# Contextual position attention in a decoder layer: selection in two halves, the position term added by VectorE, the table one group ahead

## The reference, cut to what matters

```
logits   = Q K^T / sqrt(32)
gates    = sigmoid(logits)
pos      = min(reverse cumulative sum of gates over the keys, 63)
table    = Q pos_emb                      # 64 values for each query
cope     = linear interpolation of table at pos
out      = softmax(logits + cope) V
```

## Time and profile before

| What | us |
|---|---|
| three runs, median (lowest to highest) | 15981.76 (15937.47 to 16006.48) |
| the profiled execution, own time | 15948.25 |
| its span, first to last instruction | 15946.6 |
| PE busy in the span | 13087.7 (82%) |
| VectorE (DVE) busy | 7428.1 (47%) |
| GpSimd (POOL) busy | 6506.6 (41%) |
| ScalarE (ACT) busy | 4470.2 (28%) |

### The profile page before, as it was taken

The page is one execution under the profiler, slowest core; times in us unless marked ns, Lnnn a source line. Parts: engine busy times, 40 slices in busy tenths (PEclk is TensorE's granted clock), DMA queues, the critical chain, the costliest instruction groups (busy, mean ns, idle before and its releaser), DMA issues. The chain is left out here.

```text
span 15946.6 us, 176609 instructions
## 1 busy us (share of the span) xinstructions
PE 13087.7 (82%) x57462; PEld 8694.1 (55%) x57462; DVE 7428.1 (47%) x13140; ACT 4470.2 (28%) x7890; POOL 6506.6 (41%) x5384
## 2 busy tenths in 40 slices
PE   8788999998668888888888888888888888888755
PEld 3553333333446666666666666666666666666622
DVE  0112222222235555555555555555555555555533
ACT  0111222221123333333333333333333333333310
POOL 0000000000026666666666666666666666666500
PEclk9888888898778888888888888888888888888866
DMA  3111000001123333333333333333333333333313
GB/s 79 46 44 26 20 20 20 20 20 32 64 62 76 76 74 74 77 78 74 76 75 75 75 78 78 75 77 74 75 74 77 78 75 76 75 75 75 74 63 100
DMA packets 1037897, 1029.79 MB, mean 65 GB/s; under 512 B 738307, under 2 KB 845571, under 8 KB 972307
## 3 DMA queue, kind: packets, MB, share of 16 engines
q1 hardware_dynamic: 964114, 1020.70, 27.1%
q10 hardware_dynamic: 73728, 8.42, 0.4%
HBM read 817.83 MB, written 210.76 MB: 65 GB/s over the span
## 5 line engine op out<-in xcount | busy, mean ns | idle before, releaser
L910 PE MATMUL c_pickps<-c_table,c_hot 128*128 128x112 f32 x16384 | 3422.2, 386 | 894.3 <-DMA c_table<-t_tables 795.5
L910 PEld LDWEIGHTS c_pickps<-c_table,c_hot 128*128 128x128 f32 x16384 | 3271.7, 258 | 985.5 <-DVE c_over L1196 872.4
L1286 POOL TENSOR_TENSOR c_total<-c_total,c_over 128x384 f32<-128x384 f32 (+3 forms) x3584 | 3282.1, 916 | 1029.8 <-DVE c_over L1196 751.4
L1286 POOL TENSOR_TENSOR c_total<-c_total,c_middle 128x1024 f32<-128x1024 f32 x512 | 1211.0, 2365 | 2944.7 <-DVE c_middle L1187 2944.7
L1173 DVE COPY_PREDICATED c_pickps<-c_upper,c_pickps 128x256 f32<-128x256 uint32 (+1 forms) x1024 | 798.9, 826 | 3042.5 <-PE c_pickps L910 3042.5
L1253 POOL IOTA c_digitrow<- 1x128 f32 x1 | 0.3, 256 | 4590.9 <-POOLq L65 4590.9
L1041 ACT ACTIVATE c_over<-c_place,c_thresholds 128x384 f32<-128x384 f32 (+3 forms) x3584 | 1589.7, 525 | 1.5 <-POOL c_place L1274 1.5
L1196 DVE TENSOR_TENSOR c_over<-c_over,c_pickps 128x384 f32<-128x384 f32 (+3 forms) x3584 | 1407.1, 452 | 0.0
L949 PEld LDWEIGHTS c_softps<-c_v,c_probs 128*128 128x128 f32 x8192 | 1206.4, 230 | 285.6 <-issue 265.2
L1024 ACT ACTIVATE c_place<-c_gateps 128x512 f32<-128x512 f32 x1024 | 608.8, 594 | 2607.5 <-PE c_gateps L885 2607.3
L949 PE MATMUL c_softps<-c_v,c_probs 128*128 128x33 f32 x8192 | 1218.4, 310 | 2.7 <-ACT c_probs L1051 2.7
(11 more groups left out here) (213 smaller groups left out, 14864.4 us busy)
## 6 DMA issues: line engine op xcount, KB each, us to landing
c_hot<-t_digits SPq DMA_DIRECT2D x512, 1024.0 KB
t_tables<-c_tablesb SPq DMA_DIRECT2D x256, 256.0 KB, 2.4
c_table<-t_tables SPq DMA_DIRECT2D x1024, 56.0 KB, 8.0
c_kb<-t_kb SPq DMA_DIRECT2D x256, 128.0 KB, 6.1
t_digits<-c_anchorrows SPq DMA_DIRECT2D x128, 256.0 KB, 2.3
a_q<-t_qa SPq DMA_DIRECT2D x128, 128.0 KB, 2.4
a_k<-t_ka SPq DMA_DIRECT2D x128, 128.0 KB, 2.5
c_ka<-t_kb SPq DMA_DIRECT2D x128, 128.0 KB, 2.3
```

The source lines that it names most:

```text
L910: mm = nc.tensor.matmul(pick_ps[:, h // 4, 0:WIDTH, r * 8:(r + 1) * 8], hot[t % 2][:, h, :], table[s][:, :, :, t * 16 + h].rearrange("p l ...
L1286: nc.gpsimd.tensor_tensor(a, a, b, ALU.add).then_inc(s_add, 1)
```

## The change

It touches `build_cope_attention` alone.

1. **Halves.** `pick`, `mux`, `product` and `gather_up` take a `part`: 0 is the first 64 queries of a step (two banks of `pick_ps`), 1 the others. Each has half the instructions (`pick`) or half the columns. `pick` of a half waits for the products of the same half of the step before.
2. **The position term.** `add_cope` goes. `top` begins with an addition of `total` to `score_ps` by VectorE, 128 x 1024, and the maximum waits for it.
3. **Tables a group earlier.** `tables`, `keep_table`, `send_tables` and `load_table` of group i+2 run in step 3 of group i, where they ran in steps 1 to 3 for group i+1. `tables` reads `q_a` in plain order, and `keep_table` reads PSUM in steps of eight columns to make the same layout. `load_table` comes behind both hot loads.
4. **Orders.** VectorE: `mux` and nine products of part 0, `compare(n+1)`, `top(n-1)`, `mux` of part 1, `top_row`, products 0 and 1 of part 1, `less`, in step 2 `near`, products 2 to 8 of part 1, `recip`. TensorE: `pick` part 1 of this step, a piece, `pick` part 0 of the next step, `turn_peak`, a piece, `bases`, a piece, `places`, `logits`, a piece, `values`, `turn_anchor`, a piece. Five gates stand in step 0, three in step 1, the two tables in step 3. ScalarE: three `aside`s with `keep_base` behind the second, in step 1 `lift`, `expo`, two `aside`s, in step 0 `lift`, `past`, `keep_anchor`, `norm`.

```diff
             def load_a(i, s):
-                after(sp, s_tableps, 2 * i)
+                after(sp, s_gateps, 8 * i)
...
             def load_table(i, s):
+                after(sp, s_pickps, 8 * i - 8)
+                sp.sem_inc(s_tablefree, 1)
                 sp.wait_ge(s_tablerows, 32 * (i + 1))
-                after(sp, s_pickps, 4 * i - 4)
...
                 if not final(i):
-                    send_tables(i + 1, 1 - s)
                     send_digits(i + 1, 1 - s)
                     load_hot(i + 1, 1 - s, 0)
-                    load_table(i + 1, 1 - s)
                     load_hot(i + 1, 1 - s, 1)
+                if not final(i, 2):
+                    send_tables(i + 2, s)
+                    load_table(i + 2, s)
...
             def tables(i, n):
...
-                nc.tensor.matmul(gate_ps[:, :].rearrange("p (l x) -> p l x", l=8), knots[:, 8 * n:8 * n + 8, :].rearrange("p m a -> p (m a)"),
-                                 q_a[:, :].rearrange("p (x l) -> p l x", l=8), start=True, stop=True).then_inc(s_tableps, 1)
+                nc.tensor.matmul(gate_ps[:, :], knots[:, 8 * n:8 * n + 8, :].rearrange("p m a -> p (m a)"), q_a[:, :],
+                                 start=True, stop=True).then_inc(s_tableps, 1)
...
-            def pick(i, s, t):
+            def pick(i, s, t, part):
                 n = 4 * i + t
-                pe.wait_ge(s_hot, n + 1)
-                if t == 0:
-                    pe.wait_ge(s_tableload, 128 * (i + 1))
-                after(pe, s_prod, PRODUCTS * n)
-                for h in range(16):
+                if part == 0:
+                    pe.wait_ge(s_hot, n + 1)
+                    if t == 0:
+                        pe.wait_ge(s_tableload, 128 * (i + 1))
+                after(pe, s_prod, PRODUCTS * (2 * n + part - 1))
+                for h in range(8 * part, 8 * part + 8):
...
             def pieces(i, t, at):
-                k = 6 * t + at
-                if k < 8:
-                    gates(i, k)
-                elif k < 10:
-                    tables(i, k - 8)
+                if t == 0 and at < 5 and not final(i):
+                    gates(i + 1, at)
+                elif t == 1 and at < 3 and not final(i):
+                    gates(i + 1, at + 5)
+                elif t == 3 and at < 2 and not final(i, 2):
+                    tables(i + 2, at)
...
-                nc.scalar.activation(table_sb[n][:, :], gate_ps[:, :], ACT.Copy).then_inc(s_tablesb, 1)
+                nc.scalar.activation(table_sb[n][:, :].rearrange("p (l x) -> p l x", l=8), gate_ps[:, :].rearrange("p (x l) -> p l x", l=8),
+                                     ACT.Copy).then_inc(s_tablesb, 1)
...
                     aside(0)
                     aside(1)
                     if behind:
                         keep_base(n - 1, 1 - x)
+                    aside(2)
                     if t == 1 and ahead:
                         lift(i + 1, 1 - s, 1)
-                    aside(2)
                     if behind:
                         expo(n - 1, 1 - x)
                     aside(3)
+                    aside(4)
                     if t == 0 and ahead:
                         lift(i + 1, 1 - s, 0)
                     if t < 3:
                         past(i, s, t + 1)
                     elif ahead:
                         past(i + 1, 1 - s, 0)
-                    aside(4)
+                    if t == 2 and ahead:
+                        keep_anchor(i + 1)
...
             def top(n, x):
+                dve.wait_ge(s_logit, n + 1)
+                dve.wait_ge(s_add, (PRODUCTS - 1) * (2 * n + 2))
+                nc.vector.tensor_tensor(score_ps[:, :, :], score_ps[:, :, :], total[x][:, :, :], ALU.add).then_inc(s_scored, 1)
                 dve.wait_ge(s_scored, n + 1)
...
-                    mux(i, s, t)
-                    if behind:
-                        top(n - 1, 1 - x)
-                    product(i, s, t, 0)
...
+                    mux(i, s, t, 0)
+                    for k in range(PRODUCTS):
+                        product(i, s, t, 0, k)
                     if t < 3:
                         compare(n + 1, 1 - x, 2 * i + (t + 1) // 2 + 1)
                     elif ahead:
                         compare(n + 1, 1 - x, 2 * i + 3)
-                    for k in range(5, PRODUCTS):
-                        product(i, s, t, k)
+                    if behind:
+                        top(n - 1, 1 - x)
+                    mux(i, s, t, 1)
+                    if behind:
+                        top_row(n - 1, 1 - x)
+                    for k in range(2):
+                        product(i, s, t, 1, k)
+                    if behind:
+                        less(n - 1, 1 - x)
                     if t == 2 and ahead:
                         near(i + 1, 1 - s)
+                    for k in range(2, PRODUCTS):
+                        product(i, s, t, 1, k)
                     if behind:
                         recip(n - 1, 1 - x)
```

More of the change, by code:

```diff
@@ L988, in step @@
                             values(n - 1, 1 - x, s)
[L989 to L998 removed]
+                    if t == 2 and ahead:
+                        turn_anchor(i + 1)
+                    pieces(i, t, 4)
+            for n in range(2):
+                tables(0, n)
             for n in range(8):
                 gates(0, n)
[L1002 to L1003 removed]
             places(0, 0)
             turn_anchor(0)
[L1006 removed]
+            for n in range(2):
+                tables(1, n)
+            pick(0, 0, 0, 0)
             quads(pe, step)
[L1008 removed]
             turn_peak(4 * last + 3, 1)
@@ L1094, in step @@
                             norm(i - 1, 1 - s, 3)
-                    aside(5)
-                    if t == 2 and ahead:
-                        keep_anchor(i + 1)
+            for n in range(2):
+                keep_table(0, n)
             for n in range(8):
@@ L1102, in _ @@
                     lift(0, 0, n // 4)
+            keep_anchor(0)
             for n in range(2):
-                keep_table(0, n)
-            keep_anchor(0)
+                keep_table(1, n)
             past(0, 0, 0)
@@ L1185, in product @@
                 elif k == 1:
-                    for b in range(4):
+                    for b in range(2):
                         ins = nc.vector.scalar_tensor_tensor(
-                            out=middle[x][:, :, b * 32:(b + 1) * 32], in0=here[:, :, b, :], scalar=-2.0,
-                            in1=pick_ps[:, b, 8, :].unsqueeze(1).to_broadcast([128, 8, 32]), op0=ALU.max, op1=ALU.mult)
+                            out=split(middle[x][:, :, mine])[:, :, b, :], in0=here[:, :, b, :], scalar=-2.0,
+                            in1=pick_ps[:, 2 * part + b, 8, :].unsqueeze(1).to_broadcast([128, 8, 32]), op0=ALU.max, op1=ALU.mult)
@@ L1300, in step @@
                         spread(i + 1, 1 - s, 0)
-                    gather_up(i, t)
+                    for part in range(2):
+                        gather_up(i, t, part)
             for k in range(LINKS):
```

140 lines of the change are left out of this document (59 added, 81 removed).

## The result

The changed kernel takes 17020.8 us (median of 4 runs, 16990.6 to 17043.4) where the kernel before takes 15994.1 on the same chip: a ratio of 1.0655, 95% interval 1.063 to 1.0679. It is slower, as forecast, but by 1027 us where 234 were forecast, and outside the range. The profiled execution has a span of 17001.0 us.

A forecast was written before the change was run, and what follows sets the result against it. No engine full, the stage runs by its waits; VectorE's chain sets the pace. Steps of 16.5, 22.0, 18.5 and 26.9 us make 83.9 a group against 82.07, +234 us: 16190 us; own range 15980 to 16450, 8 in 10 15500 to 16650.

The forecast's parts named there:

- VectorE's work: VectorE's instructions over a whole group: 55.6 us of work, 8.4 more than before.
- The hot wait: Step 3, VectorE before `compare`, for the next group's first hot load: 10.5 us idle a group, against 7.1 before.
- `over` in step 1: Product 2 of step 1: VectorE stands 4.1 us for ScalarE's `over`, late because the fifth gate's `aside` precedes `lift` and `past`.
- GpSimd: 8 more instructions a step, 9.4 us more a group: busy 60.3 of 84, hidden, not waited for at `top`.
- the 77 us: `keep_table`'s strided PSUM read on ScalarE: taken at 0.60 us; at 1.2 it would add 0.6 a group, 77 us.
- Rival C: Hot loads issued close together share their way: up to +9.4 us a group, 17380 us; at a third, 16580; chance 0.09.
- `values` on TensorE: The matmuls that `recip` waits for, at each step's end: 1.97 us, ending 4.33 after `less` starts.
- the waits before `recip`: End of each step but step 2: VectorE waits 1.7 to 4 us for TensorE's `values`.
- Those before `top_row`: VectorE before `top_row`: 1.0 us each step, because `turn_peak` is queued behind half a `pick`.
- The table a group ahead: Table's transfers leave the hot load's way: `pick` no longer waits 0.8 us a group, the load shortens by 1.0.
- The 0.8 of step 3: Step 3 after `compare`: 0.8 us added (0 to 1.4) for TensorE being slower after the pause.

The follow-up runs named there:

- The order of step 3 alone: Changed kernel with, in step 3, VectorE's `compare` moved behind `recip` and TensorE's next `pick` behind `values`: 15971.7 us, ratio 1.0008.
- parts tried alone: Kernel before with one part of the change: tables a group ahead, 15715.1 us; VectorE's addition for TensorE's product, 16794.2 us.
- the addition alone: Kernel before with VectorE adding `total` in place of TensorE's product with the identity, whole `pick`, old orders: 16794.2 us, ratio 1.0516.
- The move: 80 already met waits ahead of VectorE's and GpSimd's loops: 16971.5 us on the changed kernel, 15522.7 us with both orders mended.
- the best order: Changed kernel, ScalarE's fifth gate behind `past`, step 3's softmax before the hot wait, loop bodies moved: 15522.7 us; with TensorE's product back, 15205.6 us.

## Why the prediction was wrong

The sign and most of the mechanism held; the sum was 83.9 us a group and the chip made 90.4. By step, mean of the traces:

| step | predicted | measured | before |
|---|---|---|---|
| 0 | 16.5 | 17.3 | 18.1 |
| 1 | 22.0 | 24.2 | 19.6 |
| 2 | 18.5 | 18.1 | 17.7 |
| 3 | 26.9 | 30.8 | 26.6 |

- **VectorE's work** was right: 55.6 predicted, 56.7 measured. The 1.1 is `compare`: its mean is 1533 ns where it was 1301, over half of them still at 1.28 us and the others at up to 2.4. The long ones lie in steps 0 and 1. GpSimd is busy beside those of step 2 as well, but the long ones go with something narrower: a GpSimd operation starts while `compare` runs, 0.1 us or more from its ends. Of 253 that had such a start 228 took over 1.4 us, of the 259 others none; in the kernel before 11 of 383, and none of 129. It is a necessary mark in both traces, not a sufficient one, and no run tested it as a cause.
- **The hot wait** was right: 10.5 predicted, 1453.7/128 = 11.4. So was the reason: the softmax stands behind it. The order of step 3 alone was worth 1049 us.
- **`over` in step 1** was right: 4.1 predicted, 491.7/128 = 3.8 measured.
- **GpSimd** at 60.3 was 56.3, not waited for. `keep_table`'s strided read of PSUM took 597 ns, as the plain read of the earlier trace rows: the 77 us by the Trainium skill's rule ("SBUF — State Buffer", "Door 1: The DMA port swizzle") did not come. What that section says of strides in PSUM, it says of matmuls; it was the prediction that took it over to ScalarE. Rival C did not occur: the two hot loads went out together,

```profile
9994.99 1.32 SPq L831 DMA_DIRECT2D c_hot<-t_digits  x2
```

  and the `compare` of the first started at 10005.72, 10.7 us later, against 12.56 before.
- **The term that failed: `values` on TensorE, and so the waits before `recip`.** It is the largest part of the miss, a third of it. The prediction took `values` at 1.97 us from the earlier trace rows, a step 2, for every step, and let 0.8 us stand for all that is slower after a pause. In the kernel before, `values` is that short in steps 0 to 2 only; in step 3 it took 3.62, on a line that was not read because the hot wait covered it. This row of TensorE before lies between the logits and the `pick` of the earlier trace rows:

```profile
10078.81 3.62 PE L949 MATMUL c_softps<-c_v,c_probs 128*128 128x33 f32 x16
```

The change took the cover away, and lengthened `values` of step 1 from 2.01 to 3.05 (mean), step 3 staying long at 3.08; half a `pick` took 3.6 instead of 3.35. The waits before `recip` are 1357.4/128 = 10.6 a group where 8.4 were predicted: 1.0 more in step 1 and 1.2 more in step 3, the same as `values` is longer there than 1.97. Those before `top_row` are 4.7 for 4.0.

  The trace also says why `values` has two durations. The stretches of these 16 matmuls in a step 2 and in a step 3 of the kernel before, with the columns of the earlier trace rows:

```profile
10059.36:10061.33 1.97, 1.97 (x18) 1.86 (x16) 1.97 (x4) 1.97 (x5) 1.89 (x2) 1.00 0.00 0
10078.81:10082.43 3.62, 3.62 (x18) 3.49 (x16) 0.00 (x0) 2.04 (x6) 2.05 (x3) 0.50 0.59 112
```

  and in two steps 3 of the changed kernel:

```profile
9655.12:9657.09 1.97, 1.97 (x19) 1.97 (x18) 0.37 (x3) 1.97 (x5) 1.66 (x5) 1.00 0.32 73
10016.64:10020.26 3.62, 3.62 (x19) 3.62 (x18) 0.10 (x1) 2.68 (x7) 2.61 (x6) 0.50 0.42 96
```

  At a granted clock of 1.00 (2.4 GHz) they take 1.97 us, at 0.50 (1.2 GHz) 3.62. In the kernel before every step 3 from the middle of the stage has the second; in the changed kernel 82 of 123 have it, and 41 the first. Transfers run beside both of the last two rows (DMA share 0.32 and 0.42), so they don't make the difference. Of the parts tried alone, the tables lowered it in step 1: with them moved out of that step `values` there is already 2.91 in the mean, with the addition alone 2.10. The price taken from step 2 was a price at full clock.
- **The term that was missing: the reload at the loop's head**, 3.1 us in every second group, 1.55 a group. Nothing in the profile before hinted at it but the 27 packets and the size of the code. That placement makes VectorE's packets is shown; that GpSimd's body is fetched in either place is seen and not understood. The move gives 49 us in one order and 266 in another: in the second 195 are the wait at the loop's head, in the first most of what it saves there comes back in later steps, which isn't explained.
- **The table a group ahead** was priced at 1.8 us a group (0.8 and 1.0) and is worth 2.0 in the old order. That this agrees so well is partly luck: 0.9 and some 0.7 of it are those two terms, and the 0.7 of step 1 wasn't among them.
- **The clock in the sum.** The 0.8 of step 3 was the only place where the clock stood, and it was taken as given. The change itself lowers it, from 0.84 to 0.74; the addition alone took it to 0.77. That the longer waits took the rest is likely, and isn't shown.

Together: +1.1 for `compare`, +2.2 for `recip`, +0.9 for the hot load, +0.7 for `top_row`, +1.55 for the loop's head, +0.9 before `less` for `base`, −0.3 for `over`, and −0.8 because what the prediction had set aside for the clock in step 3 shows up among these waits: +6.3 of the +6.5. The range failed by the same mistake: its bounds held the steps to 0.5 us each, although `values` was priced from a step at full clock in every step, and the clock had a bound in step 3 alone.

## What to carry to other kernels

When an order is changed so that a wait goes, read the durations of everything that the wait covered, in that very step, not in one where the engine runs freely: an engine that was slow for free becomes slow on the path. Do the work that doesn't hang on a late load before the wait for it, and don't take "useless" matmuls from a TensorE that waits: in the best order here the product with the identity was worth 317 us, the addition that it spares VectorE included. If a loop body grows, count its instructions on each engine and where they lie.

## What the runs showed of the hardware

- TensorE's granted clock follows what is left for it to do: 0.84 before, 0.77 with the product alone taken away, 0.87 with ten useless products in its place, each time as the mean of 64 groups.
- VectorE's loop body of 369 instructions brought 333 packets on the instruction queue at places 442 to 811, and 28 at 517 to 886. In the changed kernel the first `mux` of a turn came 3.1 us late. With every body in two pieces, 338 packets remained, and GpSimd still stood 2.7 us behind its branch.
- `values`, the same 16 matmuls, took 1.88 us in step 0 and 3.62 in step 3 of the kernel before, each the mean of all groups: the first at a granted clock of 1.00, the second at 0.50.
- VectorE's `compare`, 128x2048, took over 1.4 us only where a GpSimd operation started while it ran: 228 of 253 such in the changed kernel, none of the 259 others.
- ScalarE read PSUM in strides at the speed of the plain read, 597 ns for 512 elements, where a TensorE product with a strided operand from SBUF took 1130, and 760 in plain order in the changed kernel.
